# Segment sums of a graph network: a selection matmul and a chained carry become transposes and a scan with a reset mask

## The chip, the cores and the metric

The kernel is one program on one core of a Trainium2 chip. Its time is the device time in microseconds (us). The core has TensorE (PE, with PEld for its weight loads), VectorE (DVE), ScalarE (ACT), GpSimd (POOL) and SyncE (SP), each with its own instruction queue.

## The reference

`x` has 100,000 nodes of 128 features; there are 25,000 edges, sorted by `dst`. Four graph layers follow each other, and each is added to `x` and layer-normalised:

```python
# 0: agg = segment_sum(edge_attr (E x 160), dst);  h = (softplus(agg @ W1.T + b1) - log 2) @ W2.T + b2;  v + h
# 1: neigh = segment_sum(x[src] * ew, dst); ws = segment_sum(ew, dst)
#    (x @ Wself.T + bself + (neigh / max(ws, 1)) @ Wneigh.T + bneigh) / 2
# 2: relu(x @ w_s + segment_sum((x @ w_n)[src], dst))
# 3: two Chebyshev convolutions (K = 3, 128 -> 256 -> 128), relu between; lap(h) = segment_sum(w * h[src], dst)
x = layernorm(x + layer(x))          # four times
```

So seven segment sums over the sorted edges are needed: one of the attributes, and six of gathered and mostly weighted rows.

## The kernel before

The edges are 196 tiles of 128, four tiles to a turn, so 49 turns (`QUADS`) to a pass. The passes follow each other, with all engines meeting between them. After a prologue (to 369 us) comes `tgt0`, the edge pass of layer 0. Then two row passes run, `src0` and `nodes`, without segment sums, and `index`, which makes indices. From 2758 us six edge passes follow: `L1` and `L2` for layers 1 and 2, and `T1`, `T2`, `LH` and `LU` for the Laplacians of layer 3. `LH` sums rows of 256 features, the others rows of 128.

An edge pass works thus. POOL gathers the rows of a turn with four indirect DMAs (line 490) into one of four slots of `rows` (`RING`); it waits only until PE has read the slot four turns back. In `tgt0` SP loads the edge attributes (160 wide, line 401) instead. DVE's `select` makes two things from the target ids, which lie in SBUF as one broadcast row `dst_row` for all slots: `cont` (line 722: does this slot's id equal that of the last slot of the tile before) and `sel` (lines 725 and 728: is row i of the tile of the same target as column j, times the edge's weight where there is one). PE's `sums` multiplies the gathered rows with `sel` (lines 1194 to 1203), which gives transposed segment sums inside a tile, in PSUM. DVE's `carry` (line 753) adds to each tile, where `cont` is one, the last column of the tile before; the four tiles of a turn are chained, and a second part of 32 or 128 features (in `tgt0` the attributes 129 to 160, in `L1` the sum of the weights, in `LH` the features 129 to 256) makes it eight instructions. In `L1` the sum of the weights is a product of `ones` with `sel` (line 1203), is transposed by eight small PE entries (line 1220), and DVE takes its maximum with 1 and its reciprocal (lines 816, 817).

PE turns or multiplies the carried sums (line 1179; 1213 and 1214 in `tgt0`; 1245 in `T2`; 1254 and 1255 in `LH`), ACT copies some of them out of PSUM, and DVE's `finish` and `norm` add the loaded row (lines 811, 821, 828, 834), take moments (761, 765), and after ACT's square root (line 1024) and a reciprocal (772) write `outb` (line 776). SP stores it. In `LU` POOL scatters `outb` to the output with four indirect DMAs a turn (line 587).

The order on each engine is written out by hand. Turn g of DVE is: `carry(g)`, `finish(g-1)`, `select(g+2)`, then `norm(g-1)` (reciprocal and `outb`). Turn g of ACT is: the copies of turn g, then `root(g-1)`. In `tgt0` DVE begins a turn with line 790 for turn g-1, and ACT computes the softplus and the root by exponentials and logarithms. Turn g of POOL in `LU` is: the gathers of g+2, then a wait for `outb` of g-1 and its scatters:

```python
def last_turn(g):
    if g.less(-LEAD).inside(QUADS):        # LEAD = 2; g.less(-2) is turn g+2
        gather("LU", g.less(-LEAD), ...)
    g = g.less(LATE["LU"])                 # LATE = 1
    out_made.wait(pool, "LU", g)
    for k in range(4): gp.indirect_dma_start(out=out, in_=outb[:, g.b, k, :], ...)
```

Of the kernel before, what the change touches and what calls it, by code (L numbers as in the profile page):

```python
# [22 lines left out]
I32 = mybir.dt.int32  # L23
ALU = mybir.AluOpType
ACT = mybir.ActivationFunctionType

P = 128
# [81 lines left out]
def gnn_kernel(nc, x, src, dst, attr, ew, W1, b1, W2, b2, Wself, bself, Wneigh, bneigh, ws, wn, G1, gb1, G2, gb2, out):  # L109
    ctx = ExitStack()  # L110
    with ctx:
# [31 lines left out]
        dst_row = sb("dst_row", [P, 1 + SLOTS], I32)  # L143
        dst_col, ew_col, lap_w, mask = (sb(n, [P, TILES]) for n in ("dst_col", "ew_col", "lap_w", "mask"))
# [7 lines left out]
        W1Tb = sb("W1Tb", [32, P])  # L152
# [16 lines left out]
        cont = sb("cont", [P, 2, 4, P], F16)  # L169
# [8 lines left out]
        sel, agg_a, agg_b, lap_in = u2, x3, x3b, y0  # L178
# [26 lines left out]
        def transfer(name, at_once=2, **n):  # L205
# [8 lines left out]
        tail_in = sem("tail_in")  # L214
        look_in = transfer("look_in", nodes=2)
# [16 lines left out]
        selected = signal("selected", {p: 1 for p in AGG})  # L232
        carried = signal("carried", {p: 8 if p in ("tgt0", "L1", "LH") else 4 for p in AGG})
        step = signal("step", {"tgt0": 2, "L1": 4, "L2": 1, "T2": 1, "LU": 1})
# [24 lines left out]
        loaded, pads, zeroed, tables_st, fixed, vstep, tstep, astep, pstep, alink, dlink, roots_in, hots, counted, row_in = (  # L259
            sem(n) for n in ("loaded", "pads", "zeroed", "tables_st", "fixed", "vstep", "tstep", "astep", "pstep",  # L260
                             "alink", "dlink", "roots_in", "hots", "counted", "row_in"))
        seam = sem("seam")
# [43 lines left out]
        def _(sp):  # L306
# [6 lines left out]
            with nc.allow_non_contiguous_dma("edge lists with an edge per partition; columns of biases"):  # L313
# [19 lines left out]
                sp.dma_start(dst_row[:, 1:1 + EDGES], row(dst).to_broadcast([P, EDGES])).then_inc(row_in, 16)  # L333
# [68 lines left out]

            def tgt0_turn(g):
                attr_load(g.less(-1))
# [6 lines left out]
            enter(sp, "tgt0")  # L411
            attr_load(Turn(0))
# [50 lines left out]
        def _(pool):  # L463
            gp = nc.gpsimd
            gp.memset(zeros[:, :], 0.0).then_inc(pstep, 1)
            gp.memset(ident[:, :], 0.0)
            gp.memset(zero_i[:, :], 0)
# [27 lines left out]
            enter(pool, "tgt0")  # L495
            def tgt0_turn(g):
# [3 lines left out]
                gather("tgt0", g, x, dst_g, xin, g.b, P, x_gathered, [(step, 2)])  # L500

# [99 lines left out]
        def _(dve):  # L601
# [13 lines left out]
            v.memset(dst_row[:, 0:1], -1)  # L615
            v.memset(dst_row[:, 1 + EDGES:], PAD).then_inc(pads, 1)
# [66 lines left out]
            v.tensor_copy(W1Tb[:, :], ps[0:32, 6, P:2 * P])  # L683
# [27 lines left out]
            def edge_pass(p, weight=None):  # L711
                two = carried.per[p] == 8

                def select(g):
# [3 lines left out]
                    summed.wait(dve, p, g, back=2)  # L718
                    carried.wait(dve, p, g, back=2)
                    r4 = dst_row[:, bass.ds(g.lin(512, 1), 512)].rearrange("p (k d) -> p k d", k=4)  # L720
                    ends = dst_row[:, bass.ds(g.lin(512), 512)].rearrange("p (k d) -> p k d", k=4)[:, :, 0:1]
                    v.tensor_tensor(cont[:, g.b], r4, ends.to_broadcast([P, 4, P]), ALU.is_equal)  # L722
                    if weight is None:
                        own = dst_col[:, bass.ds(g.lin(4), 4)].unsqueeze(2).to_broadcast([P, 4, P])
                        i = v.tensor_tensor(sel[:, g.b], r4, own, ALU.is_equal)
                    for k in range(4 if weight is not None else 0):
                        c = bass.ds(g.lin(4, k), 1)
                        i = v.tensor_scalar(sel[:, g.b, k, :], r4[:, k, :], dst_col[:, c], weight[:, c],  # L728
                                            ALU.is_equal, ALU.mult)
                    i.then_inc(selected.sem, 1)  # L730

                def carry(g):
# [11 lines left out]
                    n = 0  # L744
                    parts = [(agg_a, 0, P)] + ([(agg_b, 2, 32 if p == "tgt0" else P)] if two else [])
                    for k in range(4):
                        for t, bk, np_ in parts:
                            if n >= len(parts):
                                carried.wait(dve, p, g, k=n - len(parts) + 1)
                            elif g.c > 0:  # L750
                                carried.wait(dve, p, g, back=1, k=carried.per[p] - len(parts) + n + 1)
                            before = t[0:np_, g.b, k - 1, P - 1:P] if k else t[0:np_, 1 - g.b, 3, P - 1:P]
# [629 lines left out]
```

## Time and profile before

| | |
|---|---|
| median of 3 runs | 5211.11 us (5210.98 to 5217.34) |
| the profiled execution | 5225.39 us, span 5223.6 us, mean granted clock 0.848 |
| PE busy | 3882.5 us, 74% of the span |
| DVE busy | 3844.4 us, 74% |
| ACT busy | 1980.8 us, 38% |
| POOL busy | 3121.9 us, 60% |
| passes, us of the span | `tgt0` 369 to 913, `src0` and `nodes` to 2757, `L1` to 3193.5, `L2` to 3513.9, `T1` to 3806.7, `T2` to 4300.8, `LH` to 4627, `LU` to the end |

Busy times are shares of the whole span. Since the passes have different limits, a share says little about one pass; the view that divides the span into stretches gives busy time by engine for each. A granted clock of 1 is 2.4 GHz on PE, 0.5 is 1.2 GHz. In a timeline a row is the start, the duration, the engine, the line of the code and the tiles; neighbouring instructions of one line are put together (x4).

### The profile page before, as it was taken

The numbers are of one execution on the slowest core, as the hardware profiler recorded it, in microseconds if no ns is written. First come the engines' busy times: TensorE is split into PE (matmuls) and PEld (weight loads), VectorE is DVE, ScalarE is ACT, GpSimd is POOL, SyncE is SP. The second block draws the span as 40 slices with busy tenths as digits, with TensorE's granted clock in tenths as the row PEclk, the third lists the DMA queues.
The fourth block names the chain that finished last, engine by engine and source line by source line (L and its number), as shares of the span: only waits on it lengthen the run. The fifth ranks groups of instructions, "written<-read, shape, count | busy, mean of one in ns | idle before, by whom it ended". The sixth has DMA issues, their size and how long they took to land. (4 is left out here: it accounts for less than half of the span.)

```text
span 5223.6 us, 81294 instructions
## 1 busy us (share of the span) xinstructions
PE 3882.5 (74%) x22848; PEld 2989.2 (57%) x22848; DVE 3844.4 (74%) x16708; ACT 1980.8 (38%) x5548; POOL 3121.9 (60%) x3596
## 2 busy tenths in 40 slices
PE   3877887677899999999996775654479988952222
PEld 1333443566688888888875665653356658852221
DVE  4988776899788888888887997985544436754545
ACT  0005444455688888888881110110123320000000
POOL 0003333888688888888874444656644426656676
PEclk9987666899899999999997887986689999975555
DMA  8002222455322222222222332434445446632221
GB/s 114 1 21 79 80 80 70 153 189 191 105 78 77 76 78 75 78 78 75 78 66 79 97 97 82 134 115 133 134 142 170 167 149 189 216 118 64 62 64 58
DMA packets 392875, 536.83 MB, mean 103 GB/s; under 512 B 163788, under 2 KB 191353, under 8 KB 392172
## 3 DMA queue, kind: packets, MB, share of 16 engines
q1 hardware_dynamic: 320300, 404.19, 24.0%
q0 software_dynamic: 72128, 127.43, 9.1%
q8 instruction: 189, 3.10, 0.2%
q14 instruction: 258, 2.11, 0.1%
HBM read 275.12 MB, written 257.83 MB: 102 GB/s over the span
## 5 line engine op out<-in xcount | busy, mean ns | idle before, releaser
L1194 PE MATMUL ps<-u,rows 128*128 128x128 f32 x2744 | 581.6, 352 | 543.2 <-DMA rows<-lap,rows_of_lap 318.1
L490 POOL DMA_INDIRECT rows<-state,rows_of_src x588 | 575.7, 979 | 481.8 <-issue 156.5
L1194 PEld LDWEIGHTS ps<-u,rows 128*128 128x128 f32 x2744 | 482.4, 249 | 661.3 <-DMA rows<-lap,rows_of_lap 310.8
L753 DVE SCALAR_TENSOR_TENSOR x<-cont,x,ps 128x128 f32<-128x128 f16 x1372 | 470.8, 343 | 380.5 <-remote 159.9
L490 POOL DMA_INDIRECT xin<-in_x_dram,dst_g x196 | 198.0, 1010 | 694.7 <-SPq L273 365.6
L490 POOL DMA_INDIRECT rows<-lap,rows_of_lap x392 | 393.4, 1004 | 332.6 <-PE ps L1194 180.9
L1024 ACT ACTIVATE sd<-mv,consts 128x4 f32<-128x4 f32 x588 | 174.9, 297 | 930.2 <-DVE mv L765 495.8
L1019 ACT ACTIVATE yTa<-ps 128x512 f32<-128x512 f32 x392 | 234.3, 598 | 728.4 <-PE ps L1179 596.4
L530 POOL TENSOR_SCALAR x<-u,negm,rs 128x128 f32<-128x128 f32 x980 | 435.3, 454 | 99.9 <-issue 64.1
L555 POOL DMA_INDIRECT lk<-node_table,look_idx x392 | 385.8, 984 | 91.6 <-issue 83.2
L1179 PE MATMUL ps<-ident,x 128*128 128x128 f32 x1372 | 251.9, 315 | 248.0 <-DVE y L834 117.7
L1333 PE MATMUL ps<-V,hT 128*128 128x128 f32 x3136 | 404.5, 282 | 5.5 <-ACT hT L1103 5.5
L864 DVE BATCH_NORM_STATS2 bn<-y 128x6 f32<-128x128 f32 x1764 | 378.6, 276 | 21.7 <-POOL y L512 21.5
L1333 PEld LDWEIGHTS ps<-V,hT 128*128 128x128 f32 x3136 | 367.1, 192 | 43.0 <-ACT hT L1103 39.7
L1340 PE MATMUL ps<-yTc,G 128*128 128x512 f32 x784 | 370.5, 595 | 1.9 <-ACT yTc L1019 1.9
L1179 PEld LDWEIGHTS ps<-ident,x 128*128 128x128 f32 x1372 | 191.3, 164 | 263.3 <-issue 175.9
L1179 PEld LDWEIGHTS ps<-ident,y 128*128 128x128 f32 x1960 | 243.2, 148 | 149.7 <-issue 135.4
L1129 ACT ACTIVATE outb<-y,off,rs 128x128 f32<-128x128 f32 x784 | 322.5, 491 | 0.4 <-DVE off L892 0.4
L1157 PE MATMUL ps<-hb 128*128 128x512 f16 (+1 forms) x1176 | 231.7, 333 | 118.2 <-DVE hb L661 118.2
L512 POOL TENSOR_TENSOR y<-xin,c0h 128x512 f32<-128x512 f32 x245 | 310.6, 1268 | 14.6 <-DMA xin<-in_x_dram 13.4
L1179 PE MATMUL ps<-ident,y 128*128 128x128 f32 x1960 | 269.3, 282 | 36.8 <-POOL y L512 34.5
L490 POOL DMA_INDIRECT rows<-state_h,rows_of_src x196 | 195.1, 996 | 162.2 <-SPq L273 58.9
(228 smaller groups left out, 10089.5 us busy)
## 6 DMA issues: line engine op xcount, KB each, us to landing
state<-outb SPq DMA_DIRECT2D x196, 256.0 KB
state_h<-hb SPq DMA_DIRECT2D x98, 512.0 KB
xin<-in_x_dram SPq DMA_DIRECT2D x196, 256.0 KB
out_dram<-outb SPq DMA_DIRECT2D x196, 256.0 KB
xin<-state SPq DMA_DIRECT2D x147, 256.0 KB
rows<-in_edge_attr_10x_dram SPq DMA_DIRECT2D x48, 320.0 KB, 3.3
state<-x3b SPq DMA_DIRECT2D x49, 256.0 KB
state<-x SPq DMA_DIRECT2D x49, 256.0 KB
```

The costliest lines, as they stand in the source:

```text
L490: gp.indirect_dma_start(out=dest[:, at, k, 0:width], out_offset=None, in_=table_, in_offset=bass.IndirectOffsetOnAxis(ap=index[:, c:c + 1] ...
L512: gp.tensor_tensor(y0[:, g.b], xin[:, g.b], all4(c0h[:, :]), ALU.add).then_inc(y0_made.sem, 1)
L530: i = gp.tensor_scalar(x3[:, g2.b, k, :], u2[:, g2.b, k, :], negm[:, g2.b, k:k + 1], rs[:, 2, g2.b, k:k + 1], ALU.add, ALU.mult)
L555: gp.indirect_dma_start(out=lk[:, g.b, 2 * j:2 * j + 2], out_offset=None, in_=node_table, in_offset=bass.IndirectOffsetOnAxis(ap=look_idx[ ...
L753: v.scalar_tensor_tensor(t[0:np_, g.b, k, :], cont[0:np_, g.b, k, :], before, ps[0:np_, bk + g.b, k * P:(k + 1) * P], ALU.mult, ALU.add)\
L864: i = v.bn_stats(bn[:, n, k, :], y[:, k, :])
L1019: a.activation(out_ap, bank(bk), ACT.Copy).then_inc(kept.sem, 1)
L1129: i = a.activation(outb[:, g5.b, k, :], y3[:, g5.b, k, :], ACT.Identity, bias=off3[:, g5.b, k:k + 1], scale=rs[:, 3, g5.b, k:k + 1])
L1179: i = t.transpose(bank(bk)[:, k, :], source[:, k, :], ident[:, :])
L1194: i = t.matmul(bank(g.b)[:, k, :], rows[:, g.r, k, 0:P], sel[:, g.b, k, :], start=True, stop=True)
L1333: i = t.matmul(bank(7)[:, k, :], hT[:, j, k, :], V02[:, j, :], start=j == 0, stop=j == 1)
L1340: i = t.matmul(ps[:, 5 + j, :], G02[:, j * P:(j + 1) * P], yTc[:].rearrange("p k d -> p (k d)"), start=True, stop=True)
```

## The change

`sel`, `cont` and the broadcast row `dst_row` go. PE transposes the gathered rows with the identity, so that edges lie along the columns; and DVE runs one scan over the 512 columns of a turn: state = same x state + row, where the u8 mask `same` is 1 where an edge has the target of the edge before. The mask is made once, in `tgt0`, by one comparison a turn, from 513 target ids that SP loads per turn. ACT multiplies the gathered rows by the edge weights in place, for turn g+2 (`weigh`), in all passes but `tgt0` and `L2`; in ACT's turn g this comes before the copies of turn g and the root of g-1 (in `T2` after the copy to `hb`, ahead of `hT`). The sum of the weights moves to `tgt0`: POOL puts the weight as a 161st column beside the attributes, it runs through the transposes and the scan as row 33 of the second part, four small PE products turn it, and DVE keeps 1 / max(., 1) in `winv` for `L1`.

```diff
+                def mark_same(g):
...
+                    dst_arrived.wait(dve, p, g)
+                    v.tensor_tensor(same[:, 512 * g.c:512 * g.c + 512], dst_in[:, g.b, 1:513], dst_in[:, g.b, 0:512],
+                                    ALU.is_equal).then_inc(same_made.sem, 1)
...
                 def carry(g):
...
+                    if p == "tgt0":
+                        ws_turned.wait(dve, p, g, back=2)
+                        same_made.wait(dve, p, g)
...
-                            v.scalar_tensor_tensor(t[0:np_, g.b, k, :], cont[0:np_, g.b, k, :], before,
-                                                   ps[0:np_, bk + g.b, k * P:(k + 1) * P], ALU.mult, ALU.add)\
-                                .then_inc(carried.sem, 1)
+                        v.tensor_tensor_scan(t[0:np_, g.b].rearrange("p k d -> p (k d)"),
+                                             same[0:np_, 512 * g.c:512 * g.c + 512], ps[0:np_, bk + g.b, :],
+                                             t[0:np_, 1 - g.b, 3, P - 1:P] if g.c else 0.0, ALU.mult, ALU.add)\
+                            .then_inc(carried.sem, 1)
...
                         first_product.wait(dve, p, g1)
                         softplus_made.wait(dve, p, g1, back=1)
                         v.tensor_scalar(hT[:, 1], bank(5), b1_col[:, :], 0.0, ALU.add, ALU.max).then_inc(softplus_in.sem, 1)
+                        ws_turned.wait(dve, p, g1)
+                        ws_max.wait(dve, p, g1, back=1)
+                        v.tensor_scalar(tmpv[:, 0, :], ps[:, 4, 0:4], 1.0, None, ALU.max).then_inc(ws_taken.sem, 1)
                     if g.inside(QUADS):
                         carry(g)
+                    if p == "tgt0" and g1.inside(QUADS):
+                        ws_taken.wait(dve, p, g1)
+                        v.reciprocal(winv[:, 4 * g1.c:4 * g1.c + 4], tmpv[:, 0, :]).then_inc(ws_max.sem, 1)
                     if g.less(LATE[p]).inside(QUADS):
                         finish(g.less(LATE[p]))
-                    select(g.less(-2))
+                    if p == "tgt0":
+                        mark_same(g.less(-1))
...
+                def weigh(g):                                   # ScalarE
...
+                    rows_in.wait(act, p, g)
+                    for k in range(4):
+                        c = 4 * g.c + k
+                        i = a.activation(rows[:, g.r, k, 0:width], rows[:, g.r, k, 0:width], ACT.Copy, scale=weight[:, c:c + 1])
+                    i.then_inc(weighed.sem, 1)
...
                 def turn(g):
                     g1, g2 = g.less(1), g.less(2)
+                    if p != "T2":
+                        weigh(g.less(-2))
...
+                        (rows_in if p == "L2" else weighed).wait(pe, p, g)
                     carried.wait(pe, p, g, back=2)
                     for k in range(4):
-                        i = t.matmul(bank(g.b)[:, k, :], rows[:, g.r, k, 0:P], sel[:, g.b, k, :], start=True, stop=True)
+                        i = t.transpose(bank(g.b)[:, k, :], rows[:, g.r, k, 0:P], ident[:, :])
...
+                        ws_taken.wait(pe, p, g, back=1)
+                        for k in range(4):
+                            i = t.matmul(ps[:, 4, k:k + 1], agg_b[32:33, g.b, k, :], ones[32:33, 0:1], start=True, stop=True)
+                        i.then_inc(ws_turned.sem, 1)
```

In SP's queue of `tgt0` the id load of turn g+2 stands ahead of the attribute load of turn g+1; in the prologue the load of the broadcast row (line 333) goes.

## Rows read from the trace of the kernel before

**Rows 1.** Stretches: tgt0, L1, L2, T1, T2, LH, LU; engine busy times.

The columns are the stretch, its length, busy us (and instructions) of PE, PEld, DVE, ACT and POOL, granted clock, share of the DMA engines, GB/s.

```profile
369.00:913.00 544.00, 430.16 (x1372) 216.19 (x1372) 403.52 (x1276) 254.01 (x346) 199.92 (x199) 0.67 0.26 77
2757.80:3193.50 435.70, 317.96 (x1862) 278.20 (x1862) 397.00 (x1620) 43.83 (x98) 190.59 (x196) 0.82 0.29 89
3193.50:3513.90 320.40, 198.82 (x1372) 182.05 (x1372) 273.89 (x982) 43.85 (x98) 194.55 (x196) 0.88 0.40 121
3513.90:3806.70 292.80, 126.17 (x588) 107.53 (x588) 150.56 (x443) 29.26 (x49) 190.51 (x196) 0.63 0.40 132
3806.70:4300.80 494.10, 467.79 (x2352) 312.97 (x2352) 211.90 (x541) 141.35 (x196) 203.82 (x196) 0.97 0.47 157
4300.80:4627.00 326.20, 282.42 (x2352) 274.57 (x2352) 218.68 (x690) 29.26 (x49) 195.12 (x196) 0.94 0.62 198
4627.00:5224.00 597.00, 148.16 (x588) 123.20 (x588) 299.49 (x1129) 14.57 (x49) 389.89 (x392) 0.53 0.20 62
```

**Rows 2.** Timeline of tgt0, two turns, all engines.

```profile
652.89 0.74 DVE L790 TENSOR_SCALAR hT<-ps,b_col 128x512 f32<-128x512 f32 x1
...
656.62 0.80 PE L1194 MATMUL ps<-u,rows 128*128 128x128 f32 x2 [3.60 <-DMA rows<-in_edge_attr_10x_dram]
...
660.22 1.13 DVE L776 TENSOR_SCALAR outb<-y,mv,rs 128x128 f32<-128x128 f32 x4
...
661.79 2.08 PE L1213 MATMUL ps<-x,W1Ta 128*128 128x512 f32 x2
...
665.90 0.75 DVE L790 TENSOR_SCALAR hT<-ps,b_col 128x512 f32<-128x512 f32 x1 [4.55 <-PE ps L1214]
```

**Rows 3.** Timeline of L1, one turn of DVE.

```profile
3004.23 0.34 DVE L753 SCALAR_TENSOR_TENSOR x<-cont,x,ps 128x128 f32<-128x128 f16 x1
...
3006.30 0.15 DVE L816 TENSOR_SCALAR tmpv<-ps 128x4 f32<-128x4 f32 x1
...
3009.64 0.66 DVE L722 TENSOR_TENSOR cont<-dst_row 128x512 f16<-128x512 int32 x1
...
3011.25 0.17 DVE L772 RECIPROCAL rs<-sd 128x4 f32<-128x4 f32 x1
...
3012.48 0.34 DVE L753 SCALAR_TENSOR_TENSOR x<-cont,x,ps 128x128 f32<-128x128 f16 x1
```

**Rows 4.** Instructions by form, whole span, and one of the prologue.

```profile
L1129 ACT ACTIVATE outb<-y,off,rs 128x128 f32<-128x128 f32 x784 | 322.5, 491 | 0.4 <-DVE off L892 0.4
...
L809 DVE SCALAR_TENSOR_TENSOR y<-ps,b2h 128x512 f32<-128x512 f32 x49 | 32.9, 672 | 0.1
...
L702 DVE RECIPROCAL x<-x 128x782 f32<-128x782 f32 x1 | 5.0, 5041 | 1.0 <-ACT x L1011 1.0
```

**Rows 5.** Timeline of LU: an outb and its scatter, then one turn.

```profile
4831.63 1.11 DVE L776 TENSOR_SCALAR outb<-y,mv,rs 128x128 f32<-128x128 f32 x4
4832.66 1.49 DVE L753 SCALAR_TENSOR_TENSOR x<-cont,x,ps 128x128 f32<-128x128 f16 x4
4833.57 1.02 POOL L587 DMA_INDIRECT out_dram<-outb,out_row  x1 [6.17 <-DVE outb L776]
...
4901.06 0.99 POOL L490 DMA_INDIRECT rows<-lap,rows_of_lap  x1 [0.30 <-DVE outb L776]
...
4904.24 0.30 ACT L1024 ACTIVATE sd<-mv,consts 128x4 f32<-128x4 f32 x1 [5.87 <-DVE mv L765]
...
4906.17 1.03 POOL L587 DMA_INDIRECT out_dram<-outb,out_row  x1 [0.30 <-issue]
...
4907.38 2.08 PE L1194 MATMUL ps<-u,rows 128*128 128x128 f32 x8 [9.43 <-DMA rows<-lap,rows_of_lap]
...
4911.40 0.99 POOL L490 DMA_INDIRECT rows<-lap,rows_of_lap  x1 [0.30 <-issue]
```

**Rows 6.** Timeline of T2: hT and the product that takes it.

```profile
4103.84 1.26 ACT L1063 ACTIVATE hT<-ps,gb_col 128x512 f32<-128x512 f32 x2 [4.13 <-PE ps L1245]
...
4105.15 1.86 PEld L1271 LDWEIGHTS ps<-V,hT 128*128 128x128 f32 x16 [0.26 <-ACT hT L1063]
```

More of the change, by code:

```diff
@@ L23 @@
 I32 = mybir.dt.int32
+U8 = mybir.dt.uint8
 ALU = mybir.AluOpType
@@ L401, in attr_load, with dst_load @@
                     sp.dma_start(rows[:, g.r, :, 0:ATTR], one(v, g)).then_inc(attr_in.of(g), 16)
+            def dst_load(g):
+                if not g.inside(QUADS):
+                    return
+                same_made.wait(sp, "tgt0", g, back=2)
+                lo, hi = max(512 * g.c - 1, 0), min(512 * g.c + 512, EDGES)
+                at = lo - (512 * g.c - 1)
+                sp.dma_start(dst_in[:, g.b, at:at + hi - lo], row(dst[lo:hi]).to_broadcast([P, hi - lo]))\
+                    .then_inc(dst_arrived.of(g), 16)
             def tgt0_turn(g):
+                dst_load(g.less(-2))
                 attr_load(g.less(-1))
@@ L495, in _, with put_weights @@
             enter(pool, "tgt0")
+            def put_weights(g):
+                if not g.inside(QUADS):
+                    return
+                summed.wait(pool, "tgt0", g, back=RING)
+                gp.tensor_copy(rows[:, g.r, :, ATTR:ATTR + 1], ew_col[:, 4 * g.c:4 * g.c + 4].unsqueeze(2))\
+                    .then_inc(ew_put.sem, 1)
             def tgt0_turn(g):
@@ L708, in dev, with edge_pass @@
                 return rs[:, n, b, k:k + 1]
-            def edge_pass(p, weight=None):
-                two = carried.per[p] == 8
-                def select(g):
+            def edge_pass(p):
+                two = carried.per[p] == 2
+                def mark_same(g):
                     if not g.inside(QUADS):
                         return
[L718 to L730, printed above, removed]
+                    if g.c == QUADS - 1:
+                        same_made.wait(dve, p, g, back=2)
+                        v.memset(dst_in[:, g.b, 1 + EDGES - 512 * g.c:513], PAD).then_inc(padded, 1)
+                        dve.wait_ge(padded, 1)
+                    dst_arrived.wait(dve, p, g)
+                    v.tensor_tensor(same[:, 512 * g.c:512 * g.c + 512], dst_in[:, g.b, 1:513], dst_in[:, g.b, 0:512],
+                                    ALU.is_equal).then_inc(same_made.sem, 1)
                 def carry(g):
@@ L741, in carry @@
                         first_product.wait(dve, p, g, back=2)
+                    if p == "tgt0":
+                        ws_turned.wait(dve, p, g, back=2)
+                        same_made.wait(dve, p, g)
                     if p == "T1":
                         more_st.wait(dve, p, g, back=2)
[L744 to L752, printed above, removed]
[L753 to L756 removed]
+                    parts = [(agg_a, 0, P)] + ([(agg_b, 2, 33 if p == "tgt0" else P)] if two else [])
+                    for n, (t, bk, np_) in enumerate(parts):
+                        carried.wait(dve, p, g, back=1, k=n + 1)
+                        v.tensor_tensor_scan(t[0:np_, g.b].rearrange("p k d -> p (k d)"),
+                                             same[0:np_, 512 * g.c:512 * g.c + 512], ps[0:np_, bk + g.b, :],
+                                             t[0:np_, 1 - g.b, 3, P - 1:P] if g.c else 0.0, ALU.mult, ALU.add)\
+                            .then_inc(carried.sem, 1)
                 def moments(g):
```

105 lines of the change are left out of this document (53 added, 52 removed).

## The prediction

> **What bounds the kernel now.** I read three things: the busy shares by stage, then one turn of each kind of pass as a timeline, then the costs of single instructions grouped by form. The page's engine totals (PE 74%, DVE 74%, POOL 60%) name no bound, because the seven edge passes have different limits. So the stretches come first [rows 1], in the order tgt0, L1, L2, T1, T2, LH, LU; 49 turns each. The rest of the span (prologue, src0, nodes, index, 2213 us) is not touched by the change but for one load.
>
> In tgt0 (544 us) two turns form a cycle [rows 2]: from the start of L790 to the sums 3.73 us (the attribute rows land), sums to the first product 5.17 at the low clock, the two products of the first layer 4.1 (L1213, L1214), and a DVE turn of 8.46 (L790 to the end of outb, 652.89 to 661.35). Half of the sum is 10.7 per turn. L1 (435.7 us) is bound by DVE: 397 us busy [rows 1], and 8.25 us from one carry to the next without a gap [rows 3]. L2 has DVE busy 5.59 per turn; LH has PE busy 5.76 per turn (282.42 over 49) [rows 1]. Under both lies POOL, whose four gathers follow each other without a gap, 5.11 in the turn shown (4901.06 to 4906.17 [rows 5]); I count 5.2 a turn. T1 has no engine above two thirds; its idle time has no owner that I can name. T2 is PE (467.8 of 494 us [rows 1]). LU (597 us) has four gathers and four scatters on POOL: 4901.06 to 4911.40, 10.34 per turn [rows 5], and takes more because POOL also waits for outb; PE there waits for the gathered rows (9.43 us in the row shown).
>
> **The change, part by part.**
>
> *Carry becomes a scan.* Four chained L753 take 1.49 us alone [rows 5] and 2.07 with the second half (8 at a pitch of 0.26, 3004.23 to 3006.30 [rows 3]). The trace shows no scan. From below: one pass over 512 columns from PSUM in a STT is 0.67 (L809). From above: the dearest DVE operation per column is the reciprocal, 5.04 us for 782 columns, so 3.3 for 512 [rows 4]. A running sum carries each result to the next element, so I put it above L809, and as it is one instruction with one entry cost, below the four that it replaces: I take 1.2, near that end. Then L1, L2, T1, LU gain 0.3 on DVE, L1 more: 0.87, since its second part goes too; tgt0 and LH have two scans, 2.4 against 2.07, and lose 0.35.
> The Trainium skill speaks against the change here: the page "DVE: opcode table, instruction layouts, handler registers and perf-mode slots", section 6 (Datapath and trigger behaviour), says that the built-in tensor_tensor_scan runs at half throughput, since its running value is led back over a bubble. With the 0.96 GHz of its page "VectorE: DVE Perf Modes", 512 columns would be an estimated 1.07 us and a fixed cost on top, so near the 1.2; no run so far shows it.
>
> *No selection on DVE.* L722 and the four L728 behind it end; in L1 they fill the 1.61 from L722 at 3009.64 to the reciprocal at 3011.25 [rows 3]. Only in tgt0 one mask instruction over 512 columns stays, about 0.6 like L722. In L1 the select covered ACT's square root of the variances (L1024, 0.30 [rows 5]); that shows now as a wait of 0.46. So 1.15 is won.
>
> *The sum of weights* moves from L1 to tgt0: L816 and L817 (0.29 [rows 3]) and 10 PE entries leave L1; tgt0's DVE gets two tiny ones, 0.35 together.
>
> *L1*: 8.25 − 0.87 − 1.15 − 0.29 = 5.94; I add 0.1 for a root that now and then waits behind a weighing on ACT. 2.2 × 48 = **−106**. *L2*: to POOL's floor, at best 5.59 to 5.2 per turn: **−20**. *LH*: eight fewer of 48 PE entries bring PE to 5.76 × 40 / 48 = 4.8, so here too POOL's floor decides: 5.76 to 5.2, **−27**. *T1*: at most 5.98 to 5.2 (−38) if DVE were its owner, nothing if not; **−8**. *T2*: ACT's hT starts at 4103.84 and lasts 1.26, PE's L1271 begins at 4105.15 behind it [rows 6]; sums and turning lie inside that time, so shortening them gives **0**. The weighing there stands behind nothing: ACT had been idle 4.13 before hT. If that cover went, it would cost 1.4 a turn.
>
> *tgt0*: sums of 16 entries become 8, 5.17 to 1.9; but the target ids now come by a load per turn ahead of the attributes in SP's queue. From below it costs nothing, if it runs beside the others. From above: it moves 256 KB where the attribute load moves 320 KB, whose whole way from L790 to PE is 3.73, so 3.0. It has no dependence on that turn and is issued first, so I take 1.0, and rows are there at 4.75. DVE's turn: 8.46 + 0.34 (scans) + 0.35 (tiny); select shrinks by 0.58, but outb behind it waits for ACT's root of which select was the cover, so this gives nothing: 9.15. The new transposed weight sums on PE must be taken before the next carry: 1.2. At the low clock (4.75 + 1.9 + 4.1 + 1.2 + 9.15) / 2 = 10.55; if the shorter sums let PE run at the high clock DVE alone would set it near 9.4. I take 10.1 against 10.7: 0.6 × 49 = **−30**.
>
> *Weighing on ACT.* Four activations over 128 columns: L1129, with two pointers, lasts 0.49 [rows 4]; the root's 0.30 [rows 5] is the other bound. Overlapped, four are 1.2 to 1.65: 1.4. In the passes bound by POOL or DVE it lies beside other work (ACT is under 30% busy in all of them [rows 1]), and costs only at the start of a pass, 1.5 × 4 = **+6**. The order of ACT's program is what counts: in turn g it weighs the rows of g+2 *before* the root of g−1. In LU POOL in turn g issues the gathers of g+2 and then waits for outb of g−1 before its scatters. Outb waits for that root, the root for the weighing, the weighing for the gathers of g+2 that were just issued. What was parallel becomes a ring. Its links: start of the gathers to landed rows, 4901.06 to 4907.38 = 6.32; weighing 1.4; root 0.35; the reciprocal with its gap 0.24 (0.17 is L772 [rows 3]); outb 1.15; from its end (4831.63 + 1.11) to the scatter at 4833.57, 0.83; four scatters, 4906.17 to 4911.40, 5.23 [rows 5]. The sum is 15.5. Forty-six turns have both gathers and scatters: 713, and some 35 for the first two gathers, the first turns and the last three scatters: 748 against 597, **+151**.
>
> *Prologue*: the broadcast of all ids is gone; the small loads before it may land up to 3 us sooner; **−2**.
>
> Sum: −106 − 20 − 27 − 8 − 30 + 6 + 151 − 2 = −36. The profiled execution took 5225.4 us (span 5223.6) and the median of the runs is 5211.1, so 5189 for a profiled execution and **5175** for the median. A measurement of this kernel tells about 0.2% (10 us) from no change.
>
> **The rivals.**
> (a) *The scan is cheap*, 0.67. L1 gains 0.53 × 48 = 25 more, tgt0 1.06 × 49 / 2 = 26 more, the passes on POOL's floor nothing: 5124. For it: all plain DVE passes over 512 columns cost 0.66 to 0.69 [rows 3, 4]. Chance 0.13.
> (b) *LU's ring is not closed*: gathers and the root overlap because the landed rows come before POOL reaches the next turn. Then LU is at POOL's 10.34, 507 + 25 = 532, −65 in place of +151: 4960. Against it: in the turn shown the scatters begin at 4906.17, before the rows of that turn's gathers are used at 4907.38 [rows 5], which the new order forbids. 0.05.
> (c) *Slower: the scan is dear.* Each microsecond above 1.2 costs L1 48 and tgt0 49; 36 / 97 puts the break-even at 1.6 us. Once DVE passes 5.2 in LH and L2 they pay too: at 3.3 it is 97 × 2.1 = 204, LH about 108 and L2 44: 5530. For it: the dependency from column to column, and that 1.49 for four short ones is already cheap. By the rule cited above the scan stays under this point. 0.13.
> (d) *The wins fail to come*: tgt0 stays at the low clock and its weight sums stall, T1 and L2 keep their unowned idle time: L1 alone is sure, and the sum is −106 + 6 + 151 − 27 = +24 at worst, 5195 to 5235. 0.17.
>
> **How the numbers follow.** The main case, scan 1.0 to 1.5 and LU 15 to 16 per turn, has 0.52 and by itself reaches from 5140 to 5205. Case (a) ends at 5124 and (d) at 5235; what lies beyond 5095 to 5245 (b, the dear end of c) is about 0.13 and some misjudged links. Faster by over 0.2% (under 5201): 0.50 of the main case, a, b and 0.02 of (d), 0.70. Within 0.2%: 0.02 + 0.07 of (d), about 0.09. Slower: 0.21.
>
> **What would show it.** tensor_tensor_scan rows with a mean near 1.2 us; L1 near 330 us and DVE still its bound; L2 and LH near 300 with gathers at a pitch of 1.3 nearly without wait; T2 unchanged at 494; tgt0 near 514; LU near 750, with DVE waiting for ACT's root, ACT's weighing waiting for the gathered rows, and POOL idle some 4.5 us before each turn's first scatter. A mean scan above 1.6 or LU under 650 makes the prediction wrong.

## The result, and the profile after

The changed kernel takes 5226.88 us (median of 7 runs, 5224.99 to 5238.52) against 5211.11 (median of 7, 5201.87 to 5224.26): a ratio of 1.0029, 95% interval 1.0016 to 1.0042. It is slower by 0.3%, where 5175 and "faster" were forecast. The profiled execution has a span of 5236.6 us against 5223.6. All ratios are of fast runs; the only slow one, 6042 us at a granted clock of 0.62, belongs to one experiment (the kernel before with the attributes early) and is left out of its ratio.

The runs of this study fell on chips of two kinds, and the kinds matter more than the change. On the chip of the first traces, and on two later ones, the kernel before takes 5211 to 5221 us (kind I below). On two others it takes 5016 and 5020 us (kind II). A ratio is always to runs of the kernel before on the same chip. On kind II the changed kernel has a ratio of 1.0104 (1.0087 to 1.0121), so the change costs more there. No chip is known to have been used at two times, so it is not shown whether a chip stays of its kind.

Each pass is measured from its first gather to the first gather of the next. The middle columns are kind I (the first traces), the last three a chip of kind II:

| pass | forecast | before I | after I | came | before II | after II | came |
|---|---|---|---|---|---|---|---|
| start and tgt0 | −32 | 910.8 | 898.1 | −12.7 | 911.8 | 898.4 | −13.4 |
| src0, nodes, index | 0 | 1847.0 | 1856.1 | +9.1 | 1851.4 | 1853.8 | +2.4 |
| L1 | −106 | 435.7 | 327.0 | −108.7 | 420.8 | 314.7 | −106.1 |
| L2 | −20 | 320.4 | 312.5 | −7.9 | 298.5 | 263.4 | −35.1 |
| T1 | −8 | 292.8 | 287.0 | −5.8 | 256.2 | 254.8 | −1.4 |
| T2 | 0 | 494.1 | 493.1 | −1.0 | 482.7 | 485.1 | +2.4 |
| LH | −27 | 326.2 | 323.7 | −2.5 | 281.4 | 264.1 | −17.3 |
| LU | +151 | 596.6 | 739.1 | +142.5 | 510.1 | 739.6 | +229.5 |
| sum | −36 (+6 for starts in it) | 5223.6 | 5236.6 | +13.0 | 5012.9 | 5073.9 | +61.0 |

These are the stretches of the changed kernel's first trace, in the order and with the columns of [rows 1]; src0 and nodes stand between the first and the second:

```profile
368.30:898.10 529.80, 366.48 (x1372) 230.12 (x1372) 403.33 (x1030) 253.98 (x346) 208.43 (x245) 0.64 0.38 104
2754.20:3081.20 327.00, 190.04 (x1176) 177.03 (x1176) 267.57 (x931) 101.44 (x294) 185.88 (x196) 0.78 0.39 119
3081.20:3393.70 312.50, 188.38 (x1176) 173.35 (x1176) 214.61 (x735) 42.81 (x98) 185.87 (x196) 0.79 0.40 124
3393.70:3680.70 287.00, 98.40 (x392) 69.81 (x392) 62.66 (x49) 87.06 (x245) 184.93 (x196) 0.53 0.41 135
3680.70:4173.80 493.10, 444.98 (x2156) 287.47 (x2156) 126.28 (x147) 193.41 (x392) 196.53 (x197) 0.97 0.48 157
4173.80:4497.50 323.70, 248.28 (x1960) 236.97 (x1960) 152.00 (x147) 107.45 (x245) 185.20 (x196) 0.90 0.64 199
4497.50:5236.60 739.10, 107.44 (x392) 70.40 (x392) 211.81 (x735) 72.09 (x245) 382.96 (x392) 0.50 0.17 50
```

The reader is to see two things. L1 went from DVE at 397 of 436 us [rows 1] to 268 of 327. And in LU no engine is busy for more than 383 of 739 us: it is a chain, not an engine.

The new instructions, grouped by form (columns as in [rows 4]):

```profile
L771 DVE TENSOR_TENSOR_SCAN x<-same,x,ps 128x512 f32<-128x512 uint8 x336 | 428.9, 1276 | 292.5 <-remote 177.4 <-PE ps L1233 60.8 <-issue 24.1
...
L1052 ACT ACTIVATE rows<-rows,lap_w 128x128 f32<-128x128 f32 x588 | 186.8, 389 | 723.3 <-DMA rows<-lap,rows_of_lap 655.6 <-DMA rows<-state,rows_of_src 58.1 <-issue 9.6
...
L771 DVE TENSOR_TENSOR_SCAN x3b<-same,x3b,ps 33x512 f32<-33x512 uint8 x48 | 59.8, 1247 | 0.0
...
L750 DVE TENSOR_TENSOR same<-dst_in 128x512 uint8<-128x512 int32 x49 | 32.3, 660 | 7.8 <-DMA dst_in<-in_dst_dram 7.8
```

The scan takes 1.28 us and the weighing 0.39 for 128 columns; the range of the prediction was 0.67 to 3.3, the value taken 1.2. A scan over 33 partitions costs nearly the same, 1.25. The mask instruction takes 0.66.

LU in the timeline of the changed kernel; against the one turn in [rows 5]:

```profile
4801.89 0.99 POOL L506 DMA_INDIRECT rows<-lap,rows_of_lap  x1 [0.30 <-issue]
...
4808.20 1.28 ACT L1052 ACTIVATE rows<-rows,lap_w 128x128 f32<-128x128 f32 x4 [13.71 <-DMA rows<-lap,rows_of_lap]
4809.39 0.28 ACT L1040 ACTIVATE sd<-mv,consts 128x4 f32<-128x4 f32 x1
...
4809.70 0.18 DVE L790 RECIPROCAL rs<-sd 128x4 f32<-128x4 f32 x1 [10.76 <-ACT sd L1040]
4809.91 1.12 DVE L794 TENSOR_SCALAR outb<-y,mv,rs 128x128 f32<-128x128 f32 x4
...
4811.86 1.02 POOL L615 DMA_INDIRECT out_dram<-outb,out_row  x1 [5.22 <-DVE outb L794]
...
4817.08 0.99 POOL L506 DMA_INDIRECT rows<-lap,rows_of_lap  x1 [0.30 <-issue]
```

Here the forecast ring can be followed link by link. The gathers start at 4801.89, ACT's weighing 6.31 later (6.32 forecast); the root 1.19 behind it (1.4), the reciprocal 0.31 on (0.35), outb 0.21 (0.24); outb ends at 4811.03 after 1.12 (1.15), the scatter begins 0.83 later (0.83), and the next gathers 5.22 behind that (5.23). The sum is 15.19 against 15.5. POOL had stood idle for 5.22 us before the scatter "<-DVE outb"; in the turn of [rows 5] that starts at 4901.06 it did not wait at all. Before the scatter at 4833.57 it had waited 6.17 us: the kernel before lost time here too, but not in every turn.

tgt0 in the timeline of the changed kernel, one turn; against [rows 2]:

```profile
647.63 0.75 DVE L808 TENSOR_SCALAR hT<-ps,b_col 128x512 f32<-128x512 f32 x1 [0.78 <-PE ps L1247]
647.73 0.44 SPq L404 DMA_DIRECT2D rows<-in_edge_attr_10x_dram  x1
...
652.59 0.47 PE L1233 MATMUL ps<-ident,rows 128*128 128x128 f32 x1 [2.93 <-DMA rows<-in_edge_attr_10x_dram]
...
654.35 1.91 PE L1246 MATMUL ps<-x,W1Ta 128*128 128x512 f32 x2
...
655.84 1.13 DVE L794 TENSOR_SCALAR outb<-y,mv,rs 128x128 f32<-128x128 f32 x4 [0.70 <-ACT rs L1070]
...
657.81 0.75 DVE L808 TENSOR_SCALAR hT<-ps,b_col 128x512 f32<-128x512 f32 x1 [0.84 <-PE ps L1247]
657.84 0.47 SPq L404 DMA_DIRECT2D rows<-in_edge_attr_10x_dram  x1
```

The ring of two turns is still there. From the issue of the attribute load (647.73) to the sums 4.86, sums 1.76, first products to L808 at 657.81 3.46, DVE's turn from L808 (647.63) to the end of outb (656.97) 9.34, then SP's store, id load and attribute load, 0.87. The sum is 20.29, the half 10.1; over the pass it is 10.4 (L808 from 382.3 to 882.9, 48 turns), where the kernel before has 10.6.

### The profile page after: what moved, and what is told of

It is laid out like the page before. It is cut to its first block and busy times, and to the rows that moved or that the text cites. A ratio compares the mean times of both kernels' runs of the same rounds, so it can differ in the third digit from the quotient of the medians.

```text
span 5236.6 us, 75511 instructions
## 1 busy us (share of the span) xinstructions
PE 3559.3 (68%) x20986; PEld 2740.7 (52%) x20986; DVE 3336.2 (64%) x13803; ACT 2280.6 (44%) x6528; POOL 3091.3 (59%) x3646
## 5 line engine op out<-in xcount | busy, mean ns | idle before, releaser
L1233 PE MATMUL ps<-ident,rows 128*128 128x128 f32 x1372 | 344.2, 357 | 813.6 <-ACT rows L1052 582.3
L506 POOL DMA_INDIRECT rows<-state,rows_of_src x588 | 556.7, 947 | 378.2 <-issue 157.9
L1233 PEld LDWEIGHTS ps<-ident,rows 128*128 128x128 f32 x1372 | 226.0, 184 | 890.2 <-ACT rows L1052 536.4
L771 DVE TENSOR_TENSOR_SCAN x<-same,x,ps 128x512 f32<-128x512 uint8 x336 | 428.9, 1276 | 292.5 <-remote 177.4
L1052 ACT ACTIVATE rows<-rows,lap_w 128x128 f32<-128x128 f32 (+1 forms) x784 | 269.7, 416 | 739.7 <-DMA rows<-lap,rows_of_lap 655.6
L1215 PE MATMUL ps<-ident,x 128*128 128x128 f32 x1372 | 252.0, 315 | 238.5 <-DVE y L857 109.5
L790 DVE RECIPROCAL rs<-sd 128x4 f32<-128x4 f32 x147 | 26.2, 178 | 538.1 <-ACT sd L1040 523.2
L615 POOL DMA_INDIRECT out_dram<-outb,out_row x196 | 195.4, 997 | 291.8 <-DVE outb L794 241.1
L1215 PEld LDWEIGHTS ps<-ident,x 128*128 128x128 f32 x1372 | 186.2, 162 | 270.8 <-DVE x L771 177.3
L1215 PEld LDWEIGHTS ps<-ident,y 128*128 128x128 f32 x1960 | 234.2, 144 | 149.1 <-issue 133.5
```

The costliest lines, as they stand in the source:

```text
L506: gp.indirect_dma_start(out=dest[:, at, k, 0:width], out_offset=None, in_=table_, in_offset=bass.IndirectOffsetOnAxis(ap=index[:, c:c + 1] ...
L615: gp.indirect_dma_start(out=out, in_=outb[:, g.b, k, :], in_offset=None, bounds_check=NODES - 1, oob_is_err=False, out_offset=bass.Indirec ...
L771: v.tensor_tensor_scan(t[0:np_, g.b].rearrange("p k d -> p (k d)"), same[0:np_, 512 * g.c:512 * g.c + 512], ps[0:np_, bk + g.b, :], t[0:np ...
L1052: i = a.activation(rows[:, g.r, k, 0:width], rows[:, g.r, k, 0:width], ACT.Copy, scale=weight[:, c:c + 1])
L1215: i = t.transpose(bank(bk)[:, k, :], source[:, k, :], ident[:, :])
L1233: i = t.transpose(bank(g.b)[:, k, :], rows[:, g.r, k, 0:P], ident[:, :])
```

## The experiments

**LU's order.** In LU ACT takes the root first and weighs after it:

```diff
-                    if p != "T2":
+                    if p not in ("T2", "LU"):
                         weigh(g.less(-2))
...
                         root(p, g1, sd_e, mv_e, sd[:, 0, g1.b, :], mv[:, 0, g1.b, :, 1], EPS1)
+                    if p == "LU":
+                        weigh(g.less(-2))
```

> The changed kernel, but in LU alone ACT weighs the rows of turn g+2 after the root of turn g-1, not before it. Ring theory (LU's 15.2 us a turn is the closed chain gathers, weighing, root, outb, scatters): the chain is cut, LU falls from 739 us to between 530 (POOL's 10.3 a turn and ends) and 600 (as before the change), the whole from 5227 to 5020 to 5090. Rival (the weighing itself or its place between the gathers and PE costs the time, not the order): LU stays above 690 and the whole above 5175. L1 to LH stay as they are in both.

Ratio 0.9648 (0.9632 to 0.9664), 4839 us, on kind II. The stretch of LU (columns as above):

```profile
4327.30:4836.50 509.20, 96.66 (x392) 76.71 (x392) 212.18 (x735) 72.08 (x245) 384.90 (x392) 0.50 0.25 73
```

LU is 509 us, 10.3 a turn: POOL's four gathers and four scatters follow each other without a gap. The expectation was written for kind I; against the changed kernel on kind II (739.6) this one edit wins 230 us.

The same chain was opened at another link, by gathers issued three turns ahead (`LEAD = 3`), with ACT's order as changed:

> The changed kernel, but in LU POOL issues the gathers three turns ahead, not two; ACT's order stays, weighing of g+2 before the root of g-1. Ring theory: the weighing now waits for gathers issued a turn earlier, so the chain is open and LU falls from 740 us to 505 to 530. Rival (weighing ahead of the root on ACT costs by itself, about 1.4 us a turn, whatever was gathered when): LU stays above 650.

```profile
4335.70:4845.40 509.70, 107.36 (x392) 70.34 (x392) 212.20 (x735) 72.09 (x245) 384.66 (x392) 0.50 0.25 73
```

Again 510 us. The weighing ahead of the root costs nothing by itself; it costs when the rows that it waits for were gathered in the same turn. The ring is shown from two sides.

**tgt0's cycle.** SP loads the attributes one turn earlier:

```diff
-                attr_load(g.less(-1))
+                attr_load(g.less(-2))
...
             attr_load(Turn(0))
+            attr_load(Turn(1))
```

> The changed kernel, but in tgt0 SP loads the attributes of turn g+2 in turn g, one turn earlier than now. Theory A (the two-turn cycle: attribute load 4.9, transposes 1.8, first products 3.5, DVE's turn 9.0, SP's issues 0.9, half of it is 10.1 a turn): the cycle is cut, DVE's own turn of 9.0 to 9.4 sets tgt0, which shortens by 35 to 55 us. Rival B (SP's load queue or the low clock sets it): less than 12 us. The other passes stay.

Ratio 0.9975 (0.9965 to 0.9984) on kind II; tgt0:

```profile
368.10:830.00 461.90, 380.77 (x1372) 242.78 (x1372) 392.19 (x1030) 254.14 (x346) 208.01 (x245) 0.64 0.43 119
```

462 us against 530 in the changed kernel there: −68, more than the 35 to 55 expected. The turn is 8.8 us (DVE busy 392 of 462). Theory A holds as to the cycle; the turn was expected at 9.0 to 9.4. DVE's turn is shorter than the 9.34 above, since that one had two waits in it, 0.23 for the weight sums and 0.70 for the root; at 602.42 in this run the second still stands, 0.71, so that the 8.8 are DVE with ACT's root.

The same edit in the kernel before:

> The kernel before, with one edit: in tgt0 SP loads the attributes one turn earlier. In the changed kernel this edit took the turn of tgt0 from 10.4 to 8.8 us. Theory A (the same two-turn cycle through the attribute load sets the kernel before): its turn falls from 10.6 to DVE's own 8.4 or 8.5 us, tgt0 is some 95 us shorter, ratio 0.980 to 0.983; then DVE's turn of tgt0 is 0.3 to 0.4 us shorter without the change than with it. Rival B (the eight products of the sums at the low clock are the next bound): 9.3 us a turn or more, less than 65 us won.

Ratio 0.9827 (0.9797 to 0.9857) on kind I; tgt0:

```profile
371.00:825.60 454.60, 377.87 (x1372) 196.66 (x1372) 401.53 (x1274) 254.00 (x346) 198.30 (x197) 0.77 0.31 92
```

455 us, 87 less than before. So the kernel before was held by the same cycle; with the cycle open, tgt0 is 7 and 9 to 10 us longer with the change (462 on kind II, 464 on kind I) than without it (455): the turn is 8.8 us with it and 8.4 without, as the sum had it that DVE's turn grows. That the gain in tgt0 comes from the shorter sums in the cycle is read from the links (5.17 us from the sums to the first product in [rows 2], 1.76 here); no run takes the sums alone.

The price of the id load ahead of the attributes, by exchanging the two in SP's queue:

```diff
-                dst_load(g.less(-2))
                 attr_load(g.less(-1))
+                dst_load(g.less(-2))
```

> The changed kernel, but in SP's queue of tgt0 the load of the attributes stands ahead of the load of the ids, not behind it. Prices the id load in the cycle of tgt0 that was put at 1.0 us in two turns. Theory A: the attributes land 0.5 us (SP's issue) to 1.0 us earlier, tgt0 is 12 to 24 us shorter. Rival B (the loads do not queue; the transfer is what it is): less than 5 us.

Ratio 0.9961 (0.9945 to 0.9976) on kind I. Stretches of tgt0, L1, T1 and LH:

```profile
367.50:859.80 492.30, 369.56 (x1372) 237.84 (x1372) 397.37 (x1030) 254.11 (x346) 208.89 (x244) 0.66 0.38 111
2704.90:3034.30 329.40, 185.39 (x1176) 172.57 (x1176) 268.85 (x931) 101.45 (x294) 186.09 (x196) 0.80 0.39 118
3350.00:3638.20 288.20, 97.16 (x392) 67.84 (x392) 62.64 (x49) 87.22 (x245) 185.39 (x196) 0.54 0.41 134
4134.60:4455.40 320.80, 240.96 (x1960) 230.21 (x1960) 152.12 (x147) 107.51 (x245) 185.77 (x197) 0.93 0.63 201
```

tgt0 is 492 us against 528 in the run below, which leaves it alone: −35, or 0.74 a turn, 1.5 in the cycle of two, where 1.0 was in the sum and 0.5 to 1.0 expected. The load is no small thing: it delayed the attributes by more than its issue of 0.4 to 0.5. From their own issue to the sums it is 3.24 us in the turn at 606.31 of this run, against 4.86 above. And 1.5 is its price only from below: more than half of the turns of this run are at 8.8, where the cycle no longer sets them.

**What bounds L1 and T1 now.** A second scan per turn in both, into a buffer that nobody reads:

```diff
+                        if p in ("L1", "T1"):
+                            v.tensor_tensor_scan(hT[:, 0]..., same[:, 512 * g.c:512 * g.c + 512], ps[:, bk + g.b, :], 0.0, ALU.mult, ALU.add)
                         v.tensor_tensor_scan(t[0:np_, g.b]...
```

> The changed kernel with a second scan of the same size in each turn of L1 and T1, whose result nobody reads. Tests what bounds the two passes after the change. Theory: L1 is DVE's (5.95 us a turn), so it grows by 48 x 1.25 = 60 us; T1 is POOL's (5.2 a turn with DVE busy 1.3), so it grows by less than 5. Rival (L1 too has come down to POOL's floor or to ACT): L1 grows by less than 30.

Stretches of tgt0, L1 and T1, from the same chip as the run above:

```profile
368.30:895.90 527.60, 367.54 (x1372) 231.07 (x1372) 403.74 (x1030) 254.10 (x346) 208.95 (x244) 0.64 0.37 104
2740.20:3118.10 377.90, 215.70 (x1176) 202.71 (x1176) 321.58 (x980) 101.40 (x294) 185.40 (x196) 0.73 0.33 103
3433.10:3721.70 288.60, 99.74 (x392) 71.64 (x392) 117.13 (x98) 88.16 (x245) 185.37 (x196) 0.51 0.41 134
```

L1 grows from 329 to 378, by 48 us or 1.0 a turn, less than the 60 expected; T1 stays (288.2 and 288.6). L1 is DVE's, T1 is not. The 1.28 us of a scan overlap with the instruction behind it (DVE's busy time grows by 52.7 us, 1.08 a turn), and a steady turn grows by 1.11, from 5.95 to 7.06. The wait of 0.36 for the root stays as it was.

**What holds L2 and LH.** Two of the four gathers a turn in L2 and T1 (half of the rows of these passes is left out):

> The changed kernel, but in L2 and T1 POOL issues two of the four gathers of each turn, so half of the rows of these passes are left out (stale rows are used in their place). Tells what sets the 5.87 us a turn in L2 and 5.7 in T1. Theory A (the gathers set it, 5.0 a turn and a wait on top): L2 falls to DVE's pace, 4.4 to 4.8 a turn, from 312 to about 235 us, and T1 from 287 to 130 to 160. Rival B (a chain of PE, ACT and DVE sets it): L2 stays above 5.5 a turn, T1 above 5.

This run fell on kind II: L2 251 us against 263, T1 133 against 255. T1 is POOL's alone. L2 hardly moves there, because the two limits lie close together: with all gathers POOL issues its 196 without a pause, 5.0 us a turn, and with half of them the turn is DVE's, 4.8. The expectation had the numbers of kind I; the same kernel on that kind follows below. With eight slots in place of four:

> The changed kernel with eight slots of gathered rows in place of four (the change freed the room). Theory A (POOL's waits in L2, T1 and LH, about 0.9 a turn over the 5.0 of four gathers, come from the depth of four): L2, T1 and LH fall to 5.0 to 5.1 a turn, 35 to 45 us each, L1 stays at 5.9 of DVE, the whole is 100 to 140 shorter. Rival B (PE, ACT and DVE do not get on while POOL issues gathers, so the waits only move): L2, T1 and LH within 10 us of now, and the stall at the second turn of a pass grows from 17 to some 35 us.

Ratio 1.0111 (1.0093 to 1.0129) on kind II: nothing won, since L2, T1 and LH are at the 5.0 us a turn of the gathers there with four slots already.

To know which came from the chip, the two kernels themselves:

> The kernel before, with nothing changed, for a trace of it on the same chip as the runs beside it. In the last four runs the passes L2, T1 and LH took 265, 255 and 264 us where the first trace of the changed kernel has 312, 287 and 324. Theory A (it is the chip: on the first one the gather passes had stalls that this one has not): this run has L2 near 275, T1 near 255, LH near 282, LU near 520, in all 5010 to 5020, and the changed kernel is then slower by about 1%. Rival B (the edits had that effect): this run is like the first trace, 320, 293, 326, 596.

> The changed kernel, with nothing changed. Theory A (chip): 5060 to 5075 us, ratio 1.009 to 1.012. Rival B (edits): the first ratio again, 1.003, and L2, T1, LH at 312, 287, 324 us.

The kernel before on kind II, stretches of L2, LH and LU:

```profile
3184.00:3482.50 298.50, 182.37 (x1372) 163.05 (x1372) 271.98 (x983) 43.72 (x98) 196.09 (x196) 0.95 0.42 130
4221.40:4502.80 281.40, 267.35 (x2352) 266.73 (x2352) 215.22 (x689) 29.30 (x49) 201.38 (x196) 0.97 0.73 230
4502.80:5012.90 510.10, 142.10 (x588) 122.38 (x588) 297.16 (x1127) 14.56 (x49) 385.43 (x392) 0.51 0.23 73
```

The changed kernel on the same chip:

```profile
3066.90:3330.30 263.40, 167.19 (x1176) 149.24 (x1176) 212.73 (x735) 42.93 (x98) 185.74 (x196) 0.90 0.48 147
4070.20:4334.30 264.10, 232.41 (x1960) 223.67 (x1960) 153.82 (x147) 111.14 (x245) 185.37 (x197) 0.96 0.77 244
4334.30:5073.90 739.60, 107.36 (x392) 70.34 (x392) 211.72 (x735) 72.08 (x245) 383.01 (x392) 0.50 0.17 50
```

Theory A: ratio 1.0104 (1.0087 to 1.0121), and it is the chip. The kernel before also has LU at 510 there, POOL's floor, so the ring costs 230 us and not 143. And POOL's floor is real on this kind, at 5.0 us a turn where 5.2 was forecast: the changed kernel's L2, T1 and LH (263, 255 and 264 us) are four gathers a turn and 10 to 19 us of ends.

What is different can be read in one line, ACT's copy of the turned rows in L2 (idle time of ACT before it, by what ended it). On kind I, then on kind II:

```profile
  remote: 114.5, 21
```

```profile
  PE ps L1215: 183.5, 49
```

On kind II each of the 49 waits ends with PE's turning (L1215), as it should. On kind I 114 us are put down to nothing on this core. The second turn of L2 shows it at its largest, in the timeline of the changed kernel on kind I:

```profile
3099.66 1.06 PE L1215 MATMUL ps<-ident,xin 128*128 128x128 f32 x4
...
3114.04 0.94 POOL L506 DMA_INDIRECT rows<-state,rows_of_src  x1 [3.17 <-remote]
3114.55 0.60 ACT L1035 ACTIVATE yTa<-ps 128x512 f32<-128x512 f32 x1 [19.43 <-remote]
```

PE has the turning at 3099.66, and ACT, which waits for it, begins at 3114.55, 14 us after its recorded end. POOL had issued gathers without a pause from 3081.2 to 3110.9, and its own wait for PE's sums ended at 3114.04. The kernel before has the same stall at the second turn of its L2, on the same kind:

```profile
3226.91 0.69 DVE L828 SCALAR_TENSOR_TENSOR y<-ps,xin 128x512 f32<-128x512 f32 x1 [17.87 <-remote]
```

The same copy of ACT on kind II waits 4.6 us:

```profile
3085.46 0.60 ACT L1035 ACTIVATE yTa<-ps 128x512 f32<-128x512 f32 x1 [4.62 <-PE ps L1215]
```

The kept traces also hold the times at which semaphores were raised, and they show what is late. The one that ACT waits for here was raised at 3114.53, the one of PE's sums at 3113.78, both some 14 us after the recorded ends. In L2 of this trace 69 of 107 recorded raises by PE come over 0.5 us after the recorded end of their product, by up to 13.9 us; on kind II none comes more than 0.02 us after it, in any pass. DVE and ACT raise theirs alike on both kinds. In tgt0 of kind I, where POOL pauses in every turn, no raise is late, and in T2 hardly any behind the second turn. So: do PE's signals come the later, the more gathers POOL issues in a row?

> The changed kernel with two of the four gathers a turn in L2 and T1 (half of the rows left out), again. If the chip is of the kind of the first trace (L1's second carry stands 23 us after the first ones): theory A (the stalls come while POOL issues gathers): L2 falls from 313 to below 260 us and T1 from 287 to below 170. Rival B (a chain without POOL): L2 above 300. If the chip is of the other kind, L2 251 and T1 133 as in the first such run.

> The changed kernel with eight slots, again. On a chip of the first kind: theory A (what PE signals comes late while POOL issues gathers, so a deeper ring gives POOL more to issue before it pauses): the stall at the second turn of L1, L2 and T2 grows from 23 to about 43 us, the steady turns of L2 and T1 stay near 5.8 or come in bursts of eight. Rival B (depth four is too shallow for the landing): the steady turns of L2 and LH fall to 5.0. On the other kind of chip: 5072 us as before.

Both fell on kind I. L2 and T1 with half of the gathers:

```profile
3071.40:3328.00 256.60, 172.15 (x1176) 154.49 (x1176) 212.45 (x735) 42.98 (x98) 92.94 (x98) 0.88 0.40 126
3328.00:3478.50 150.50, 87.49 (x392) 62.84 (x392) 62.65 (x49) 86.83 (x245) 92.71 (x99) 0.66 0.64 214
```

L2 is 257 us against 312, at 4.8 in nearly every turn; T1 150 against 286. ACT's second copy in L2, with half of the gathers, and then with eight slots:

```profile
3088.00 0.60 ACT L1035 ACTIVATE yTa<-ps 128x512 f32<-128x512 f32 x1 [7.64 <-remote]
```

```profile
3154.18 0.60 ACT L1035 ACTIVATE yTa<-ps 128x512 f32<-128x512 f32 x1 [33.38 <-issue]
```

The wait before it is 7.6 us with half of the gathers, 19.4 with four slots and all of them, and 33.4 with eight slots. From the start of the pass to its first pause POOL issues 12, 24 and 44 gathers in a row. On kind II the same wait is 4.5, 4.6 and 5.3 us, so the delay itself is some 3, 15 and 28 us. L1 to LH lose 89 us in all with eight slots (L1 349.5, L2 329.9, T1 295.5, T2 518.9, LH 336.1, against 327.1, 311.8, 286.1, 493.3 and 322.4 in the run with both edits below, on the same chip, which leaves these passes alone). Behind the start the turns of L2 and LH are 5.7 and 5.8 us on average, against 5.8 and 6.0: far from 5.0. Theory A holds as far as the delay grows with the gathers in a row, and the rival falls: a deeper ring makes it worse. Whether it is POOL's issuing or the traffic of the gathers that delays PE's signals was not told apart; on kind II L2 moves more bytes a second (147 GB/s against 124) without any delay. That a signal comes through only when POOL pauses does not hold; with eight slots ACT's copy at 3154.18 starts while POOL goes on issuing.

**The better version.** Both edits that gained, together:

> The changed kernel with both edits that gained alone: in LU ACT takes the root of turn g-1 before it weighs the rows of g+2, and in tgt0 SP loads the attributes one turn earlier. If the gains add, they are 230 and 67 us of the changed kernel's 5070: 4765 to 4780 us, ratio 0.950 to 0.953. If one takes from the other (they lie in different passes, so nothing should), above 4790.

Kind II: 4774.04 us, ratio 0.9515 (0.9500 to 0.9531). The gains add.

> The changed kernel with root first in LU and the attributes a turn earlier in tgt0, again. On a chip of the first kind: LU about 570 us as in the run with the weighing last everywhere, tgt0 463, LH back at 321: 4990 to 5005 us, ratio 0.956 to 0.960. On the other kind 4774 and 0.9515 as before.

Kind I: 4988.21 us, ratio 0.956 (0.954 to 0.958). Its tgt0 and LU, 464 and 565 us against 530 and 739 in the changed kernel's first trace (LU is 174 us shorter there, 230 on kind II):

```profile
367.90:832.20 464.30, 383.11 (x1372) 244.54 (x1372) 392.38 (x1030) 254.14 (x346) 208.43 (x245) 0.64 0.44 118
4423.20:4988.30 565.10, 100.81 (x392) 74.17 (x392) 215.41 (x735) 73.84 (x245) 384.48 (x392) 0.50 0.22 66
```

With the weighing last in every pass but T2:

> The changed kernel with the attributes of tgt0 loaded a turn earlier and, in all passes but T2, ACT weighing the rows of g+2 as the last thing of its turn, behind the copies of g and the root of g-1. Theory (only in LU is the order on a closed chain): the same time as with the edit in LU alone, 4765 to 4785 us, ratio 0.950 to 0.953, L1, T1 and LH within 3 us. Rival (root and copies wait behind the weighing in L1, T1 and LH too): 5 to 25 us shorter in L1 and LH.

Ratio 0.9778 (0.9756 to 0.9801) on kind I, a miss. LU is 571 us, as wanted, and L1 is within 2 us (331.1 against 329.4), T1 is 7 us longer (294.9 against 288.2), and LH takes 430.6 us against 320.8. In its timeline (ACT, then PE):

```profile
4349.23 0.60 ACT L1113 ACTIVATE y<-ps 128x512 f32<-128x512 f32 x1 [5.70 <-PE ps L1291]
...
4349.73 1.69 ACT L1053 ACTIVATE rows<-rows,lap_w 128x256 f32<-128x256 f32 x4
...
4358.95 0.60 ACT L1113 ACTIVATE y<-ps 128x512 f32<-128x512 f32 x1 [7.53 <-PE ps L1291]
...
4359.44 1.69 ACT L1053 ACTIVATE rows<-rows,lap_w 128x256 f32<-128x256 f32 x4
...
4361.19 0.33 PE L1234 MATMUL ps<-ident,rows 128*128 128x128 f32 x1 [3.42 <-ACT rows L1053]
```

In LH the copy that stands in front (L1113) waits for the product of turn g, so the weighing of g+2 starts only then; PE's order has the sums of g+2 ahead of the product of g+1, so they wait for the weighing, and the next product for them. It is a ring of 9.7 us in the turn shown and 8.3 on average, made by the same edit that opens the one in LU. Neither of the two places, first or last in ACT's turn, is right for both passes; a place between the root and the copies was not tried.

## Why the prediction was wrong

The forecast was a small sum of two large terms and several small ones, and its sign was wrong. Both large terms were right: L1 (−106 forecast, −108.7 came) and LU's ring (+151, +142.5; 15.5 a turn against 15.2). The scan was put at 1.2 and measured 1.28. T2 at 0 (−1.0) held too. T1 at −8 (−5.8) came out near by luck: its turns behind the start did not get shorter (5.6 us before, 5.8 after), and on kind II it gave −1.4. The rule of the Trainium skill cited in the prediction, "DVE: opcode table, instruction layouts, handler registers and perf-mode slots", section 6 (half throughput for the scan), agrees with the trace: the 1.07 us estimated from it for 512 columns, with a fixed cost on top, is near the measured 1.28. The rival in which the scan is as cheap as L809 is out.

The three steps that failed are all among the small terms. Together they came 65 us short (tgt0 19, L2 12, LH 25, src0 and nodes 9), and the other terms gave 16 back:

1. "To POOL's floor": *L2 −20, LH −27* brought −8 and −2. The sum read the turns of the kernel before from busy times, DVE's 5.59 and PE's 5.76, and let them fall to POOL's 5.2 as if nothing else stood in between. On the chip of the traces PE's late signals stood there. LH takes 6.0 us a turn before and after. L2 was DVE's before in most turns (the median is 5.75, and 5.74 on kind II) and 5.9 on average; the change relieved DVE, but the late signals keep the average at 5.8. The stall at the second turn of L2 stays too, 23.7 us from carry to carry before and 23.0 after, against 9.8 and 8.9 on kind II. The trace before had shown it: of the 160 us of idle time "<-remote" before DVE's carry 87 are in T1, 32 in LH and 41 in LU, and L2 has the 17.9 us before L828 shown above. I had counted such time as without an owner in T1, and let L2 and LH gain anyway. On kind II, where the stalls are absent, the same step gave −35 (5.7 to 5.0 us a turn) and −17 (5.4 to 5.0).
2. *tgt0, "I take 10.1 against 10.7": −30* brought −12 with the start. The cycle at the low clock had been worked out as 10.55, and 10.1 lay about in the middle between this and the 9.4 of a high clock. The clock did not rise (granted share 0.67 [rows 1], 0.64 after), and the mean turn is 10.4. The 10.7 of the kernel before was that of one pair of turns; its mean is 10.6. Three of the links were off as well, partly against each other: the wait for the weight sums, put at 1.2, is 0.23 us before L811, the first products, put at 4.1, take 3.46, and SP's three issues, 0.87, were missing. The id load, put at 1.0, costs 1.5 or more.
3. *src0 and nodes, 0* brought +9 on kind I and +2 on kind II. It is not the change: in src0 a turn takes either 8.2 or 8.5 us, and the kernel before has both in its second trace; in the other traces with the change in it this stretch takes 1844 to 1854 us, where the kernel before has 1847 to 1853. Such a mode is within the 0.2% that were called noise, but a sum of −36 leaves little room for it.

Of the rivals it is (d), the wins that fail to come, that took place: it gave 5195 to 5235 and had 0.17. Its case "T1 and L2 keep their unowned idle time" is what happened, only that it still counted on the −27 of LH, which did not come either, and that tgt0 brought a part. (b) is out by two experiments: the ring is closed, and opening it at either of two links gives 510 us on kind II. On kind II the result would have been outside (d) as well, as LU's loss there is 230 us, since the kernel before has LU at the floor.

## What to carry to other kernels

When an engine's program takes on work for a later turn, put it behind everything that a slower queue waits for in this turn, and then follow each ring through it: gathers of g+2, weighing, root, outb, scatters is a ring because POOL issues both ends and the weighing waits for gathers of the same turn. One line of order was worth 230 us on one kind of chip and 174 on the other, and the same line in another pass cost 110. And a pass with idle time that no engine owns gave next to nothing back here when its busy engine was relieved (LH −2 of 27 us, L2 −8 of 20); price such a gain at zero until an experiment (half of the gathers) shows who owns it.

## What the runs showed of the hardware

On chips of one kind, what PE signals arrives late while POOL issues indirect DMAs one behind the other: ACT's wait at the second turn of L2 is 7.6, 19.4 and 33.4 us with 12, 24 and 44 gathers in a row, where it is 4.5 to 5.3 on the other kind, and L2 and LH take 5.8 and 6.0 us a turn in place of 5.0. On chips of the other kind POOL issues all 196 gathers of L2 in a row and nothing of it shows; the kernel before takes 4% less there and the changed one 3%. It is PE's semaphores that are raised late, not DVE's or ACT's. Whether PE itself works late then or only its signals are held is open: its recorded starts lie before the wait, but the ends of matmuls are modelled.

A scan of 512 columns takes 1.25 us on 33 partitions and 1.28 on 128; two in a row follow each other at 1.2, and the instruction behind a scan starts 1.2 us after it (2900.00 and 2901.19 in L1 of the first trace).
